# Copies of turned probabilities after the score tiles of three and four key tiles, on ScalarE instead of VectorE

## The chip, the cores and the metric

The kernel runs on one core of one Trainium2 chip. The metric is the device time of one execution in microseconds (us). A core has five engines that run their own instruction streams and meet only at semaphores: TensorE (PE in the rows: PE is the matmul, PEld the weight load that overlaps it), VectorE (DVE), ScalarE (ACT), GpSimd (POOL) and SyncE (SP, which issues the DMAs).

## The reference

The input x is 32 images of 192 channels and 32 x 32 points. Three layers follow; the change touches the second.

```python
x = _L0_conv_ref(x, ...)                  # channel attention, 8 heads, plus x
t = _to_tokens(x)                         # 32 x 1024 tokens x 192
t = t + _L1_attn_ref(_ln_t(t), Wq, Wk, Wv)
t = t + _L1_ffn_ref(_ln_t(t), W1, b1, W2, b2)
x = _from_tokens(t, x)
...
def _L1_attn_ref(x, Wq, Wk, Wv):          # H = 6 heads, d = 32
    att = jnp.einsum('bqhd,bkhd->bhqk', q, k) * scale
    causal = jnp.tril(jnp.ones((T, T), dtype=bool))
    att = jnp.where(causal, att, -jnp.inf)
    att = jax.nn.softmax(att, axis=-1)
    out = jnp.einsum('bhqk,bkhd->bqhd', att, v)
```

The attention is causal over 1024 tokens. Cut into 8 query tiles of 128, query tile number q needs q + 1 key tiles of 128.

## The kernel before

**Units and slots.** A unit is one head and one query tile of one image: 48 units to an image, 1536 in all. The function `attention` runs over slots. It is called six times: for five groups of 6 images, and for a last pair. Between the calls stands the feed-forward layer (`group_tail`), which the change doesn't touch. In slot n the scores of unit n are made (line 659, and 661 for the causal mask), and the probabilities of unit n - 3 are turned, that is transposed (line 673), so that the product with V can follow (line 693). `TILES = [(1, 7), (3, 5), (0, 6), (2, 4)]` gives the query tiles: in blocks of six slots, even slots have the small query tile of the pair and odd slots the big one, for three heads. With the key tiles counted, four blocks (24 slots, twice in an image) run 2/8, 4/6, 1/7, 3/5. So where a small unit of three or four key tiles is turned, three slots later, the scores of a big unit are being made: of 8 key tiles in slots 1 and 25 of an image, of 6 in slots 9, 11, 33 and 35, of 7 in slots 13 and 37, of 5 in slots 21, 23, 45 and 47.

**One slot, engine by engine.** Each engine's program is written out slot by slot, and each engine runs its own strictly in that order:

- TensorE: scores of unit n, then transposes of unit n - 3 into a bank PT0 or PT1 of PSUM, then, in some slots, the product with V, then one step of the front of the next image (its layer 0, layer norm and projections, lines 560 to 636), spread over slots 0 to 44.
- VectorE: the row maximum of unit n (line 1172, `nmax`), then its copies of turned probabilities from PT into `work` (line 373), then its part of the front (among it BN_STATS at line 1046).
- ScalarE: Exp of unit n (line 915; it ends with an instruction of its own that reads the accumulated row sum), then its copies (line 919, which run in `pt_copy`), then its part of the front (lines 843 to 876).

**Chunks and banks.** The turned probabilities of a unit go into chunks of at most four key tiles (512 columns). Units of up to four key tiles have one chunk, larger ones two. Chunks take the banks PT0 and PT1 in turn (`i % 2`), so the transposes of chunk i + 2 wait until the copy of chunk i has emptied its bank:

```python
pe.wait_ge(pt_free[i % 2], after(g, 0, PT_IMG, i // 2))
```

A small unit turned in slot n is chunk i. In slot n + 1 a big unit follows with chunks i + 1 and i + 2, and chunk i + 2 needs the bank of the small one. Behind it on TensorE are the product with V, a front step and the scores of slot n + 2. Other waits that matter: scores of unit n wait for the Exp of unit n - 2, whose tile S they overwrite.

**Who copies.** `by_act` decides. Before, ScalarE copies every second chunk of a unit (`chunk[3] > 0`) and VectorE every first one.

Of the kernel before, what the change touches and what calls it, by code (L numbers as in the profile page):

```python
# [67 lines left out]
def qtile(n):  # L68
    return TILES[n // 6 % 4][n % 2]
# [91 lines left out]
def hybrid_kernel(nc, x, wa, wb, wv, wpt, bp, temp, w3, w1, b1, w2, b2, out):  # L161
# [5 lines left out]
    with ctx:  # L167
# [193 lines left out]

        def by_act(i, chunk):

            return chunk[1] == "p" and chunk[3] > 0

        def pt_copy(eng, copy, g, images, i):

# [457 lines left out]
        def _(act):  # L825
# [74 lines left out]
            def attention(g, images, fronts):  # L900
                for n in range(last_slot(images) + 1):
                    for j in batches_at(images, n, OT_AT):
                        act.wait_ge(pv_made, after(g, 0, KI, BATCH * (j + 1)))
                        if j >= 1:

                            act.wait_ge(t1_step, after(g, 0, 3 * NBI, 3 * (j - 1) + 2))
                        A(oT[:, :], OUT[0:CH, :], ACT.Copy).then_inc(oT_made, 1)
                    if n < UNITS * images:

                        act.wait_ge(max_made, after(g, 0, UNITS, n + 1))  # L910
                        if n >= 4:
                            i = max(i for i, c in enumerate(CHUNKS[images]) if c[1] == "p" and c[2] == n - 4)
                            act.wait_ge(pt_full[i % 2], after(g, 0, PT_IMG, i // 2 + 1))
                        w = P * (qtile(n) + 1)
                        A(PS[n % 2][:, n // 2 % 2, 0:w], S[:, n % 2, 0:w], ACT.Exp, bias=nmax[:, n % MAXES:n % MAXES + 1],  # L915
                          accum_out=rowsum[:, sum_col(n):sum_col(n) + 1]).then_inc(exp_made, 1)
                    for i, c in chunks_at(images, n):
                        if by_act(i, c):
                            pt_copy(act, lambda o, x: A(o, x, ACT.Copy), g, images, i)  # L919
                    fronts_at(n, lambda name, u: front_part(name, g, u + 1), order, fronts)  # L920
                    if images == GS and EARLY.get(n, "").startswith("norm"):
                        act.wait_ge(rstd2_made, after(g, 0, 4, 4))
                        norm_z2(0, g * GS, int(EARLY[n][-1]), zcat0)
                    if images == GS and EARLY.get(n, "").startswith("turn"):
                        k = int(EARLY[n][-1])
                        put_z2(0, g * GS, k, FB[k % 2])
# [57 lines left out]
        def _(dve):  # L984
# [183 lines left out]
            def attention(g, images, fronts):  # L1168
                for n in range(last_slot(images) + 2):
                    if n < UNITS * images:  # L1170
                        dve.wait_ge(scores_full, after(g, 0, UNITS, n + 1))
                        v.tensor_reduce(nmax[:, n % MAXES:n % MAXES + 1], S[:, n % 2, 0:P * (qtile(n) + 1)], AX.X, ALU.max,  # L1172
                                        negate=True).then_inc(max_made, 1)
                    for i, c in chunks_at(images, n):
                        if c[1] == "p" and not by_act(i, c):
                            pt_copy(dve, v.tensor_copy, g, images, i)

                    for i, c in chunks_at(images, n):
                        if c[1] == "o":
                            add_to_t1(g, i, c[2])  # L1180
                    fronts_at(n, lambda name, u: front_part(name, g, u + 1), later, fronts)
                    if images == GS and n in EARLY:
                        part = EARLY[n].removeprefix("next_")
                        b = int(part != EARLY[n])
                        if part == "stats0" and b:
                            dve.wait_ge(ln2_step, after(g, 0, 16, 16))
                            alone(dve)
                        if part.startswith("stats"):
                            stats2(b, range(4 * int(part[-1]), 4 * int(part[-1]) + 4))
                        elif part == "aggregate":  # L1190
                            aggregate2(g * GS + b)
# [158 lines left out]
```

## Time and profile before

| | |
|---|---|
| median of 3 runs | 4680.67 us (4678.06 to 4683.2) |
| the profiled execution, its own time | 4680.1 us |
| its span in the profile | 4678.3 us |
| TensorE busy (matmul) | 4079.7 us, 87% |
| TensorE weight loads | 2975.4 us, 64% |
| VectorE busy | 3329.6 us, 71% |
| ScalarE busy | 2690.2 us, 58% |
| GpSimd busy | 363.1 us, 8% |
| share of the chain that ended last | TensorE 62%, VectorE 15%, issue 14%, ScalarE 4% |
| mean granted TensorE clock | 0.977 of full |

The busy times are of the whole span. Matmuls overlap each other, so the busy share of TensorE is an upper view of its work. The chain is followed back from the last instruction, at each step to what released it.

### The profile page before, as it was taken

Reading aid. Unit: us, or ns where it says so; the run is one execution under the profiler, and the core shown is the slowest. Engines: PE = TensorE matmul, PEld = TensorE weight load, DVE = VectorE, ACT = ScalarE, POOL = GpSimd, SP = SyncE. Lnnn points to the kernel's source line nnn. Section 1 sums busy time; section 2 is a strip of 40 time slices with the busy share of each in tenths; the row PEclk is TensorE's granted clock in tenths of the full one; section 3 lists DMA queues with packets and bytes.
Section 4 is the critical chain, followed back from the end, with each engine's and each line's share of the span. In section 5 each row is a group of like instructions: output and inputs, shape, how many; then the busy total and the mean of one; then the engine's idle time right before and its main releaser. Section 6 shows DMA issues by size and latency. Waiting matters only on the chain.

```text
span 4678.3 us, 114637 instructions
## 1 busy us (share of the span) xinstructions
PE 4079.7 (87%) x39208; PEld 2975.4 (64%) x39208; DVE 3329.6 (71%) x6327; ACT 2690.2 (58%) x5901; POOL 363.1 (8%) x374
## 2 busy tenths in 40 slices
PE   3899988878999888999998979999888989988888
PEld 2667665566667646766675566666646667665665
DVE  3677777767777767777777777777767777776776
ACT  1565556555656655555556545565655555556555
POOL 1000002000000120000002000000110000002000
PEclk8999999999999999999999999999999999999999
DMA  1211111011111201111111011122101111111011
GB/s 43 60 37 35 35 35 35 0 47 37 35 35 41 48 10 41 35 35 35 35 38 33 0 49 35 35 51 46 35 0 41 35 35 35 42 35 28 0 41 42
DMA packets 48635, 160.95 MB, mean 34 GB/s; under 512 B 12420, under 2 KB 12934, under 8 KB 48006
## 3 DMA queue, kind: packets, MB, share of 16 engines
q1 hardware_dynamic: 48134, 154.39, 13.8%
q8 instruction: 300, 4.92, 0.4%
q14 instruction: 201, 1.65, 0.1%
HBM read 28.52 MB, written 25.17 MB: 11 GB/s over the span
## 4 chain that ended last, share of the span: by engine, by line
PE 62%; DVE 15%; issue 14%; ACT 4%; POOL 2%; DVEq 1%; DMA 1%; ACTq 0%; SPq 0%; POOLq 0%
PE PT L673 10%; PE OUT L693 10%; PE S L659 5%; PE PT L790 5%; DVE nmax L1172 4%; PE S L718 4%; DVE work L373 4%; PE S L619 2%; PE FR L619 2%; PE S L761 2%; PE FR L567 2%; PE S L567 2%; DVE XT L1054 1%; PE FR L626 1%; PE S L626 1%
## 5 line engine op out<-in xcount | busy, mean ns | idle before, releaser
L915 ACT ACTIVATE work<-S,nmax 128x256 f32<-128x256 f32 (+7 forms) x1536 | 1137.2, 741 | 1127.6 <-DVE nmax L1172 1059.5
L1172 DVE TENSOR_REDUCE nmax<-S 128x1 f32<-128x256 f32 (+7 forms) x1536 | 1156.7, 753 | 806.3 <-PE S L661 788.3
L673 PE MATMUL PT<-ident,work 128*128 128x128 f32 x6912 | 1103.7, 280 | 225.8 <-DVE work L373 197.0
L673 PEld LDWEIGHTS PT<-ident,work 128*128 128x128 f32 x6912 | 745.6, 142 | 433.7 <-DVE work L373 261.0
L373 DVE COPY work<-PT 128x512 f32<-128x512 f32 (+3 forms) x1536 | 893.6, 582 | 42.5 <-PE PT L673 35.0
L659 PE MATMUL S<-KS,QS 128*128 128x512 f16 (+3 forms) x1152 | 323.1, 335 | 61.2 <-ACT work L915 28.8
L661 PE MATMUL S<-causal,identb 128*128 128x128 bf16 x1536 | 339.7, 221 | 0.0
L659 PE MATMUL S<-odd 128*128 128x512 f16 (+3 forms) x1152 | 315.6, 328 | 22.9 <-ACT work L915 21.5
L919 ACT ACTIVATE work<-PT 128x512 f32<-128x512 f32 (+3 forms) x768 | 330.5, 430 | 3.4 <-PE PT L673 3.4
L693 PE MATMUL OUT<-work,odd 128*32 128x128 f32 x6912 | 303.6, 276 | 0.0
L1206 DVE TENSOR_REDUCE gm<-S 128x1024 f32 (+1 forms) x180 | 220.0, 1222 | 117.2 <-PE S L761 116.9
L693 PE MATMUL OUT<-work,V 128*32 128x128 f32 x6912 | 303.0, 275 | 0.0
L915 ACT ACTIVATION_READ_ACCUMULATOR work<-S,nmax 128x1 f32 x1536 | 301.1, 196 | 0.0
L718 PE MATMUL S<-odd,W1b 128*128 (+1 forms) x1080 | 256.9, 390 | 49.6 <-ACT work L958 41.3
L761 PE MATMUL S<-odd,W1b 128*128 (+1 forms) x1080 | 292.0, 379 | 0.0
L958 ACT ACTIVATE work<-S,sc 128x512 f32<-128x512 f32 x360 | 254.4, 782 | 50.1 <-PE S L718 49.6
L693 PEld LDWEIGHTS OUT<-work,odd 128*32 128x32 f32 x6912 | 235.6, 110 | 39.8 <-issue 31.2
L693 PEld LDWEIGHTS OUT<-work,V 128*32 128x32 f32 x6912 | 234.3, 110 | 39.8 <-issue 32.1
L790 PE MATMUL PT<-W2b,work 128*128 128x192 f16 x2880 | 247.5, 247 | 9.0 <-DVE odd L1259 8.8
L790 PEld LDWEIGHTS PT<-W2b,work 128*128 128x128 f16 x2880 | 238.8, 98 | 23.7 <-DVE odd L1259 9.9
L1251 DVE SCALAR_TENSOR_TENSOR work<-work 128x1024 f16<-128x1024 f32 x180 | 218.4, 1225 | 28.3 <-ACT work L965 24.2
L661 PEld LDWEIGHTS S<-causal,identb 128*128 128x128 bf16 x1536 | 151.6, 99 | 126.6 <-issue 11.8
(205 smaller groups left out, 6018.9 us busy)
## 6 DMA issues: line engine op xcount, KB each, us to landing
X<-in_x SPq DMA_DIRECT2D x32, 768.0 KB, 5.3
odd<-hi_z SPq DMA_DIRECT2D x128, 192.0 KB, 4.2
odd<-odd SPq DMA_DIRECT2D x128, 192.0 KB, 4.2
out_y<-work SPq DMA_DIRECT2D x64, 384.0 KB, 3.6
QS<-hi_z SPq DMA_DIRECT2D x64, 192.0 KB, 3.9
QS<-odd SPq DMA_DIRECT2D x64, 192.0 KB, 4.0
KS<-hi_z SPq DMA_DIRECT2D x64, 192.0 KB, 4.5
KS<-odd SPq DMA_DIRECT2D x64, 192.0 KB, 4.6
```

The source lines that it names most:

```text
L373: copy(PTS[m % 2][:, m // 2 % RING, P * c0:P * (c0 + k)], PT[i % 2][:, 0:P * k]).then_inc(pt_free[i % 2], 1)
L659: mm(S[:, n % 2, c0:min(w, c0 + 512)], q, KS[u % 2][:, h, c0:min(w, c0 + 512)], start=True, stop=c0 + 512 < w)
L661: mm(S[:, n % 2, w - P:w], identb[:, :], causal[:, :], start=False, stop=True).then_inc(scores_full, 1)
L673: last = tr(bank[:, P * (j - c0):P * (j - c0) + P], PS[m % 2][:, m // 2 % 2, P * j:P * j + P], ident[:, :])
L693: last = mm(OUT[32 * hh:32 * hh + 32, o:o + P], V[u % 2][:, j, D * h:D * h + D], PTS[k % 2][:, unit_of(k, hh) // 2 % RING, P * j:P * j + P ...
L718: last = mm(bank, W1b[:, j, P * (i % 6):P * (i % 6) + P], rhs[:, j, :], start=(j == 0), stop=(j == 2))
L761: last = mm(bank, W1b[:, j, P * m:P * m + P], Z2[:, b, hf, j, :], start=False, stop=(j == 2))
L790: last = mm(PT[tp % 2][:, C * t:C * t + C], HS[:, hf, part, m, o:o + P], W2b[:, m, :], start=(m == 0 and part == 0), stop=(m == MH - 1 and ...
L915: A(PS[n % 2][:, n // 2 % 2, 0:w], S[:, n % 2, 0:w], ACT.Exp, bias=nmax[:, n % MAXES:n % MAXES + 1], accum_out=rowsum[:, sum_col(n):sum_co ...
L919: pt_copy(act, lambda o, x: A(o, x, ACT.Copy), g, images, i)
L958: A(H[:, i % MH, :], Y[i % 4], ACT.Gelu, bias=rb1[:, i % MH:i % MH + 1], scale=r1).then_inc(gelu_made, 1)
L1172: v.tensor_reduce(nmax[:, n % MAXES:n % MAXES + 1], S[:, n % 2, 0:P * (qtile(n) + 1)], AX.X, ALU.max, negate=True).then_inc(max_made, 1)
```

## The change

The first chunks of the units with query tiles 2 and 3 (three and four key tiles, 384 and 512 columns, one chunk each) are copied by ScalarE. An image has 12 such units, the kernel 384: 192 of each size. The instruction, its data and its waits stay the same; it stands in the same slot, on another engine.

```diff
         def by_act(i, chunk):
 
-            return chunk[1] == "p" and chunk[3] > 0
+            return chunk[1] == "p" and (chunk[3] > 0 or qtile(chunk[2]) in (2, 3))
```

On TensorE nothing moves. On ScalarE, in slot 25 of an image, the new copy comes behind the Exp of the unit with eight key tiles (128x1024) and ahead of the Exp of slot 26 (128x256). A minus is a row of before, a plus one of the change:

```order
 L915 ACTIVATE work,rowsum<-S,nmax 128x1024
-L910 REGISTER_ALU
-L913 REGISTER_ALU
+L369 REGISTER_ALU
+L919 ACTIVATE work<-PT 128x384
+L910 REGISTER_ALU
 L915 ACTIVATE work,rowsum<-S,nmax 128x256
```

The copy of 384 columns stands between two Exps that followed each other before.

On VectorE, the same slot 25 (with slot 24 ahead of it) in the program before: the maximum and the copy of slot 24, the maximum of slot 25, its copy, and the layer norm statistics of the front.

```order
L1171 REGISTER_ALU
L1172 TENSOR_REDUCE nmax<-S 128x1
L369 REGISTER_ALU
L372 REGISTER_ALU
L373 COPY work<-PT 128x512
L1171 REGISTER_ALU
L1172 TENSOR_REDUCE nmax<-S 128x1
L369 REGISTER_ALU
L373 COPY work<-PT 128x384
L353 REGISTER_ALU x2
L1046 BN_STATS stats<-T 128x6 x4
```

The same place in the changed program:

```order
L1171 REGISTER_ALU
L1172 TENSOR_REDUCE nmax<-S 128x1
L369 REGISTER_ALU
L372 REGISTER_ALU
L373 COPY work<-PT 128x512
L1171 REGISTER_ALU
L1172 TENSOR_REDUCE nmax<-S 128x1
L353 REGISTER_ALU x2
L1046 BN_STATS stats<-T 128x6 x4
```

The statistics now follow the maximum at once; the copy of 384 columns is gone from VectorE.

## Rows read from the trace of the kernel before

**Rows 1.** The page, costliest groups: busy us, mean ns | idle before, releasers.

```profile
L673 PE MATMUL PT<-ident,work 128*128 128x128 f32 x6912 | 1103.7, 280 | 225.8 <-DVE work L373 197.0
```

**Rows 2.** Groups by shape: copies on VectorE (L373) and ScalarE (L919).

```profile
L373 DVE COPY work<-PT 128x512 f32<-128x512 f32 x960 | 654.7, 682 | 38.1 <-PE PT L673 30.8 <-issue 1.2
...
L919 ACT ACTIVATE work<-PT 128x512 f32<-128x512 f32 x192 | 112.9, 588 | 0.0
...
L919 ACT ACTIVATE work<-PT 128x384 f32<-128x384 f32 x192 | 93.0, 484 | 0.0
```

**Rows 3.** Timeline, slots 1 and 2 of an image: start us, duration us, instruction.

```profile
1974.12 0.55 DVE L373 COPY work<-PT 128x384 f32<-128x384 f32 x1
...
1974.72 0.33 PE L673 MATMUL PT<-ident,work 128*128 128x128 f32 x1 [0.35 <-DVE work L373]
...
1975.25 0.19 ACT L915 ACTIVATION_READ_ACCUMULATOR work<-S,nmax 128x1 f32 x1
1975.34 0.48 ACT L851 ACTIVATE XT<-S 128x386 f32<-128x386 f32 x1
```

**Rows 4.** Timeline of the same image, slots 9 and 10, then 13 and 14.

```profile
1993.10 0.19 ACT L915 ACTIVATION_READ_ACCUMULATOR work<-S,nmax 128x1 f32 x1
...
1993.56 0.38 PE L673 MATMUL PT<-ident,work 128*128 128x128 f32 x2
...
2003.50 0.44 PE L673 MATMUL PT<-ident,work 128*128 128x128 f32 x2 [0.65 <-DVE work L373]
...
2003.79 0.19 ACT L915 ACTIVATION_READ_ACCUMULATOR work<-S,nmax 128x1 f32 x1
```

**Rows 5.** Timeline of the same image, slots 25 to 27.

```profile
2029.80 0.33 PE L673 MATMUL PT<-ident,work 128*128 128x128 f32 x1 [0.44 <-DVE work L373]
...
2030.32 0.19 ACT L915 ACTIVATION_READ_ACCUMULATOR work<-S,nmax 128x1 f32 x1
...
2031.29 0.22 PE L661 MATMUL S<-causal,identb 128*128 128x128 bf16 x1
...
2031.97 1.22 DVE L1172 TENSOR_REDUCE nmax<-S 128x1 f32<-128x1024 f32 x1
...
2032.20 0.41 PE L673 MATMUL PT<-ident,work 128*128 128x128 f32 x2 [0.69 <-ACT work L915]
```

**Rows 6.** Timeline of the same image, slots 33 to 35.

```profile
2046.65 0.44 PE L673 MATMUL PT<-ident,work 128*128 128x128 f32 x2
2046.83 0.21 ACT L915 ACTIVATION_READ_ACCUMULATOR work<-S,nmax 128x1 f32 x1
...
2047.58 0.22 PE L661 MATMUL S<-causal,identb 128*128 128x128 bf16 x1
...
2047.84 0.33 PE L673 MATMUL PT<-ident,work 128*128 128x128 f32 x1
```

**Rows 7.** Timeline of the same image, slots 37 and 38.

```profile
2056.35 0.19 ACT L915 ACTIVATION_READ_ACCUMULATOR work<-S,nmax 128x1 f32 x1
...
2056.41 0.38 PE L673 MATMUL PT<-ident,work 128*128 128x128 f32 x2
```

**Rows 8.** Timeline, slots 45 to 47 of the image before it.

```profile
1967.95 0.33 PE L673 MATMUL PT<-ident,work 128*128 128x128 f32 x1 [0.38 <-DVE work L373]
...
1968.16 0.19 ACT L915 ACTIVATION_READ_ACCUMULATOR work<-S,nmax 128x1 f32 x1
...
1968.69 0.22 PE L661 MATMUL S<-causal,identb 128*128 128x128 bf16 x1
...
1969.10 0.41 PE L673 MATMUL PT<-ident,work 128*128 128x128 f32 x2 [0.20 <-DVE work L373]
```

**Rows 9.** Windows, slots 16 to 24: us; PE, PEld, DVE, ACT, POOL busy; clock; DMA.

```profile
372.13:394.63 22.50, 20.05 (x188) 16.49 (x187) 15.07 (x38) 11.45 (x31) 0.00 (x0) 0.92 0.01 2
...
2005.83:2026.67 20.84, 18.39 (x189) 15.28 (x187) 14.70 (x38) 11.45 (x31) 0.00 (x0) 1.00 0.00 1
...
4065.21:4087.71 22.50, 20.05 (x189) 16.49 (x188) 14.89 (x38) 11.45 (x31) 0.00 (x0) 0.92 0.01 2
```

## Prediction

> **What bounds the kernel now.** I first read the page's groups. The busiest engine is TensorE, and where it stands still in front of the transposes (line 673) it is nearly always for a VectorE copy out of PT: 197.0 of 225.8 us [rows 1]. That looks like a case for taking copies off VectorE. But the row doesn't say what VectorE did before the copy, nor when ScalarE could have made it. For that I read the timeline of one whole image, slot by slot, and set beside each copy that moves (a) when TensorE needs the bank again, and (b) when ScalarE would reach the copy. The same places in the other images gave the same distances to within some 0.01 us where TensorE waits, so one image stands for all.
>
> What the reader is to see is the chain inside an odd slot. The scores of a big unit end; VectorE takes the maximum; from there the ways part. VectorE copies the small unit's chunk at once, and in slot 2 TensorE starts 0.05 us after that copy's end (1974.12 + 0.55 = 1974.67, start 1974.72) [rows 3]. ScalarE starts the Exp of the big unit at the same moment as VectorE its copy, and reaches its own copies only when the Exp is through; in slot 1 the read of the row sum starts at 1975.25, half a microsecond after TensorE already has the bank [rows 3]. The kernel is bound by this latency from slot to slot, and by TensorE's own work where front steps fill the slots, not by the sum of work on VectorE (71% busy) or ScalarE (58%).
>
> **The change part by part.** It takes 192 copies of 512 columns at 0.682 us [rows 2] and 192 of 384 columns at 0.55 [rows 3] off VectorE: 237 us. It adds 192 at 0.588 and 192 at 0.484 to ScalarE [rows 2]: 206 us. Neither sum is on the path. No transpose, DMA or semaphore is added.
>
> A sentence on a rule: the Trainium skill, ScalarE: Activation LUTs, Rules for kernel authors, budgets about 0.3 us and 0.83 ns per element for an ACTIVATE. By it the two copies would be estimated at 0.72 and 0.62 us, 0.14 more than the rows have, and the eight late places counted below would cost some 34 us more. The rows decide here, since they have this very copy on this very engine.
>
> *When the copy is done on ScalarE.* The instruction after the row-sum read starts 0.09 to 0.10 us after the read's start (1975.25, then 1975.34) [rows 3]. So the copy ends at the read's start + 0.10 + 0.48 (384 columns) or 0.59 (512), and TensorE starts 0.05 later: read + 0.63 or + 0.74. Subtracting the present start of the transposes that need the bank gives the new stall in each image:
>
> - slot 1 (384): 1975.25 + 0.63 - 1974.72 = 1.16 [rows 3]
> - slot 9 (512): 1993.10 + 0.74 - 1993.56 = 0.28 [rows 4]
> - slot 13 (512): 2003.79 + 0.74 - 2003.50 = 1.03 [rows 4]
> - slot 25 (384): 2030.32 + 0.63 - 2029.80 = 1.15 [rows 5]
> - slot 33 (512): 2046.83 + 0.74 - 2046.65 = 0.92 [rows 6]
> - slot 37 (512): 2056.35 + 0.74 - 2056.41 = 0.68 [rows 7]
> - slot 45 (384): 1968.16 + 0.63 - 1967.95 = 0.84 [rows 8]
> - slot 21: the same subtraction gives under 0.1; I count 0.08.
>
> In the other four (slots 11, 23, 35, 47) a long product with V stands between the two chunks, and the bank is needed only 0.7 to 2.3 us after ScalarE is done: nothing, as long as that product covers it; without it, they would cost like their neighbours.
>
> *What is absorbed.* A stall pushes back the product with V, the front step and the scores of slot n + 2, and with them the next maximum, Exp and copies: most later waits of TensorE start from those scores and move along whole. Only waits on something made before the stall shrink. VectorE is now ahead by the copy it lost. I find three places:
>
> - Slot 45. The mask matmul of slot 47 moves from 1968.69 to 1969.53, and slot 47's transposes, which so far wait until 1969.10 for a VectorE copy, can follow at 1969.58: 0.48 of the 0.84 is left for TensorE [rows 8].
> - Slot 25. The mask matmul of slot 27 moves from 2031.29 to 2032.44; its transposes from 2032.20 to about 2032.49, only 0.29. But the maximum of slot 27 starts at 2031.97 now because VectorE is behind, and then at 2032.44 + 0.22 + 0.04 = 2032.70. What follows to slot 31 hangs on that maximum: 0.73 [rows 5]. This is where taking 0.55 us off VectorE helps.
> - Slot 33. The mask matmul of slot 35 goes from 2047.58 to 2048.50, the transposes from 2047.84 to 2048.55: 0.71 of 0.92 [rows 6].
>
> The others are carried in full. What is queued behind the new copies on ScalarE (front copies of lines 851 to 871, the small Exp) is up to 0.6 us later, but its readers come at least a slot later, and the small Exp waits today for a maximum that VectorE will deliver earlier. I count nothing for it; if that cover is gone, the front steps on TensorE slip by up to the same 0.6 in the slots with a new copy.
>
> Sum per image: 0.48 + 0.28 + 1.03 + 0.08 + 0.73 + 0.71 + 0.68 = 3.99 us, times 32 = 128 us. Slot 1 has no such copy in the first image of each of the six calls: 26 x 1.16 = 30 us. Together **158 us**.
>
> *The clock.* From slot 16 to slot 24 an image takes 20.84 us at a granted clock of 1.00; in 8 of the 32 images it takes 22.50 us at 0.92 [rows 9], that is, TensorE ran for a short time at 1.2 instead of 2.4 GHz: 1.66 us for each such fall. TensorE stood still for 20.84 - 18.39 = 2.45 us in that stretch. Elsewhere in attention the profile has hardly a fall. The change makes new stalls of that kind: 0.35 + 1.16 in slot 2, 0.65 + 1.03 in slot 14, 0.44 + 1.15 in slot 26 [rows 3 to 5]. Their price has bounds: no fall, 0; a fall in every image at two of the three, 64 x 1.66 = 106 us. I take the rate of the row that is nearest, 8 at each of the three places: 24 x 1.66 = **40 us**.
>
> The sum is 4680.1 (the profiled execution's own time) + 158 + 40 = 4878 us. The profiled time is 0.6 below the median of the runs, which changes nothing.
>
> **The rivals.**
>
> *Forecast: slower, by the late bank* (chance 0.72), near 4878. Its own range is 4820 to 4940.
>
> *Partly absorbed* (0.14). The late bank is real, but VectorE, with 237 us less to do, and the slack of the front steps take back more than I found: only the three longest stalls at slots 1, 13 and 25 count, at half: 32 x (1.03 + 1.15) / 2 + 26 x 1.16 / 2 = 50 us, without falls: 4730. For it speaks that VectorE is behind in slots 25 to 31; against it that in slots 1 to 12 TensorE has only waits that start from the delayed scores.
>
> *Slower still* (0.08). Nothing is absorbed (4.98 x 32 + 30 = 190 us), and the clock falls twice in each image (106 us): 4976.
>
> *Faster, by relief of VectorE* (0.04). VectorE is behind from slot 25 to 31, and TensorE waits there for its copies. If the bank of the moved chunk isn't what holds TensorE, the stretch gets shorter by the copy that leaves, 0.55 x 32 = 18 us: 4662. It decides if ScalarE delivers the chunk no later than VectorE now, so if the Exp is over within the 0.55 us of VectorE's copy. The rows have the row-sum read 0.52 us after TensorE's present start [rows 5], so it misses by 1.15. The Trainium skill, Perfetto Trace Analysis, Optimizing Scalar/DVE Operations, says that where VectorE is saturated, moving work to ScalarE may make sense; by that rule this rival would be the likely one. No row here shows VectorE saturated over an image.
>
> *No change that can be told* (0.02): the stalls hidden behind front steps, as in slots 11 and 35, everywhere: 4680.
>
> **How the numbers follow.** The predicted time is the forecast's, 4878. The low end, 4800, has three quarters of the 158 us and no fall (4680 + 119); the high end, 4940, has nothing absorbed and 42 falls (190 + 70). Below it lie the partly absorbed case and the two others, above it part of the last. A measurement of this kernel tells about 0.2% (9 us) from no change. Faster by more: 0.04; within: 0.02; slower by more: 0.94.
>
> **What the profile of the changed kernel would show.** The copies of line 373 fall from 1536 to 1152 and those of line 919 rise from 768 to 1152, with 0.48 and 0.59 us for the new ones. TensorE's wait in front of line 673 has ScalarE's copy (line 919) as its main releaser, with about seven waits an image; its sum rises by 100 to 190 us. The timeline of an image shows the stalls at slots 2, 14, 26, 34, 38 and 46 at about the lengths above, and an image takes 4 to 5 us longer plus the falls. VectorE and ScalarE wait longer for scores. More short falls of the clock stand between slots 0 and 31. I am wrong if the stalls are there but the images aren't longer (absorbed), if line 919 isn't the releaser, or if the clock falls at nearly every one of the new stalls.

## The result, and the profile after

| | before | after |
|---|---|---|
| median of 5 runs each | 4680.67 us (4678.06 to 4684.71) | 4846.58 us (4844.26 to 4852.95) |
| ratio | | 1.0354, 95% interval 1.034 to 1.0368 |
| the profiled execution, span | 4678.3 us | 4845.1 us |
| mean granted TensorE clock | 0.977 | 0.965 |

The change makes the kernel slower by 165.9 us; the prediction said 198 (4878), range 4800 to 4940.

The page of the kernel after, its engines and the groups that answer to [rows 1]. Columns as before: busy us, mean ns of one, idle before, and what ended it.

```profile
span 4845.1 us, 114637 instructions
...
PE 4122.1 (85%) x39208; PEld 3010.4 (62%) x39208; DVE 3137.6 (65%) x5943; ACT 2850.5 (59%) x6285; POOL 363.1 (7%) x374
...
L673 PE MATMUL PT<-ident,work 128*128 128x128 f32 x6912 | 1123.3, 282 | 355.0 <-ACT work L919 236.3
```

VectorE is busy for 192 us less and ScalarE for 160 more (the durations sum to 237 and 206, but rows of successive instructions overlap by about 0.1 us), and TensorE still waits longer: in front of the same transposes it stands 355.0 us instead of 225.8, and the releaser has changed from VectorE's copy to ScalarE's. The waits of the same kernel split it:

```profile
PE PT L673 <- ACT work L919: 236.3, 188, 1.8
...
PE PT L673 <- DVE work L373: 109.7, 221, 0.9
```

Each row has the total in us, the number of waits and the longest. 188 waits of 1.26 us in the mean for ScalarE's copies are new, six an image where I had said seven; those for VectorE fall from 197.0 to 109.7. ScalarE's copies by shape, to be set against [rows 2]:

```profile
L919 ACT ACTIVATE work<-PT 128x512 f32<-128x512 f32 x384 | 226.0, 589 | 0.0
...
L919 ACT ACTIVATE work<-PT 128x384 f32<-128x384 f32 x384 | 185.2, 482 | 1.4 <-PE PT L673 1.0
```

The new copies last what the old ones of that shape did, 0.59 and 0.48 us. They aren't slow, they are late. The timeline of slots 1 and 2 of an image, which answers to [rows 3]:

```profile
2041.33 1.11 ACT L915 ACTIVATE work<-S,nmax 128x1024 f32<-128x1024 f32 x1 [1.07 <-DVE nmax L1172]
2042.34 0.19 ACT L915 ACTIVATION_READ_ACCUMULATOR work<-S,nmax 128x1 f32 x1
2042.43 0.48 ACT L919 ACTIVATE work<-PT 128x384 f32<-128x384 f32 x1
...
2042.96 0.33 PE L673 MATMUL PT<-ident,work 128*128 128x128 f32 x1 [1.50 <-ACT work L919]
```

ScalarE has stood idle for 1.07 us for the maximum, then runs the Exp, and only then the copy. In the kernel that copies ahead of the Exp (below), the chunk is ready within the time of that wait. TensorE stands for 1.50 us instead of 0.35: 1.15 more, where the prediction had 1.16.

**Stretch by stretch.** The windows below cut an image where slots begin (at the mask matmul). First the kernel before, slots 0 to 3, 11 to 15, 23 to 27, 27 to 33, 33 to 39, and 39 to the next image's slot 0. Columns: window, us, busy of PE, PEld, DVE, ACT and POOL, granted clock, DMA share, GB/s.

```profile
1971.34:1976.60 5.26, 4.91 (x52) 3.72 (x51) 3.73 (x6) 3.47 (x11) 0.00 (x0) 1.00 0.64 153
1995.40:2005.27 9.87, 8.91 (x129) 7.36 (x127) 5.93 (x13) 3.88 (x11) 1.00 (x1) 1.00 0.01 2
2023.01:2031.29 8.28, 7.57 (x97) 5.84 (x95) 6.06 (x21) 3.72 (x9) 0.10 (x1) 1.00 0.38 95
2031.29:2044.78 13.49, 10.00 (x105) 6.58 (x103) 12.97 (x27) 8.22 (x19) 4.93 (x4) 1.00 0.01 4
2044.78:2059.41 14.63, 14.51 (x155) 9.76 (x153) 9.85 (x15) 10.05 (x25) 0.00 (x0) 1.00 0.01 2
2059.41:2077.60 18.19, 17.48 (x207) 13.59 (x205) 13.71 (x24) 12.75 (x30) 0.00 (x0) 1.00 0.58 125
```

The same stretches of the kernel after, in images where the clock stood at 1.00:

```profile
2038.43:2044.84 6.41, 4.91 (x53) 3.71 (x51) 3.27 (x5) 4.05 (x13) 0.00 (x0) 1.00 0.51 117
1952.77:1963.67 10.90, 8.91 (x129) 7.36 (x127) 4.75 (x11) 4.92 (x13) 1.06 (x1) 1.00 0.01 2
1981.56:1990.99 9.43, 7.56 (x97) 5.83 (x95) 5.75 (x19) 5.21 (x14) 1.63 (x2) 1.00 0.32 85
1990.99:2004.05 13.06, 9.81 (x104) 6.59 (x103) 12.30 (x25) 7.47 (x15) 3.45 (x3) 1.00 0.01 2
2004.05:2020.09 16.04, 14.54 (x156) 9.74 (x153) 8.33 (x12) 11.42 (x28) 0.00 (x0) 1.00 0.01 2
2020.09:2038.43 18.34, 17.12 (x207) 13.57 (x206) 12.72 (x22) 13.29 (x32) 0.00 (x0) 1.00 0.60 132
```

TensorE's busy time is the same in each pair but the fourth and the last, where it differs by 0.2 and 0.4; its time standing still is what grows.

| slots | before | after | more | the prediction's terms for it |
|---|---|---|---|---|
| 0 to 3 | 5.26 | 6.41 | 1.15 | 1.16 |
| 11 to 15 | 9.87 | 10.90 | 1.03 | 1.03 |
| 23 to 27 | 8.28 | 9.43 | 1.15 | 1.15 |
| 27 to 33 | 13.49 | 13.06 | -0.43 | 0.73 - 1.15 = -0.42 |
| 33 to 39 | 14.63 | 16.04 | 1.41 | 0.71 + 0.68 = 1.39 |
| 39 to the next slot 0 | 18.19 | 18.34 | 0.15 | 0.48 |

The two stretches with the small terms, slots 9 to 11 and 15 to 23, are 0.33 and 0.14 longer by the starts of their mask matmuls (0.28 and 0.08 in the prediction). The fourth line is the relief of VectorE: in a stretch in which VectorE is busy for 12.97 of 13.49 us, part of the stall comes back. Two runs below place it at the copy of slot 25: slots 27 to 33 take 13.06 us where the units of three key tiles alone are moved, and 13.48 where those of four alone are.

The prediction counted nothing for what is queued behind the new copies on ScalarE. The stretches agree: slots 3 to 9, which have no new copy, take 14.45 us in both kernels, and no other stretch grows by over 0.06 us more than its computed stalls.

### The profile page after: what moved, and what is told of

The parts are those of the page before. It is cut to its first block, busy times and chain, and to the rows that moved or that the text cites. A ratio compares the mean times of both kernels' runs of the same rounds, so it can differ in the third digit from the quotient of the medians.

```text
span 4845.1 us, 114637 instructions
## 1 busy us (share of the span) xinstructions
PE 4122.1 (85%) x39208; PEld 3010.4 (62%) x39208; DVE 3137.6 (65%) x5943; ACT 2850.5 (59%) x6285; POOL 363.1 (7%) x374
## 4 chain that ended last, share of the span: by engine, by line
PE 60%; issue 14%; DVE 14%; ACT 8%; POOL 2%; DVEq 1%; DMA 1%; ACTq 1%; SPq 0%; POOLq 0%
PE PT L673 11%; PE OUT L693 10%; DVE nmax L1172 5%; PE S L659 5%; PE PT L790 4%; PE S L718 4%; ACT work L919 3%; PE S L619 2%; DVE work L373 2%; PE S L761 2%; PE FR L567 2%; PE S L567 2%; ACT work L915 2%; PE FR L619 2%; PE FR L626 1%
## 5 line engine op out<-in xcount | busy, mean ns | idle before, releaser
L673 PE MATMUL PT<-ident,work 128*128 128x128 f32 x6912 | 1123.3, 282 | 355.0 <-ACT work L919 236.3
L673 PEld LDWEIGHTS PT<-ident,work 128*128 128x128 f32 x6912 | 755.8, 144 | 563.1 <-ACT work L919 291.9
L373 DVE COPY work<-PT 128x512 f32<-128x512 f32 (+2 forms) x1152 | 658.5, 572 | 42.5 <-PE PT L673 35.5
L919 ACT ACTIVATE work<-PT 128x512 f32<-128x512 f32 (+3 forms) x1152 | 538.3, 467 | 8.4 <-PE PT L673 8.0
L693 PE MATMUL OUT<-work,V 128*32 128x128 f32 x6912 | 320.9, 286 | 0.0
L693 PE MATMUL OUT<-work,odd 128*32 128x128 f32 x6912 | 320.8, 286 | 0.0
L693 PEld LDWEIGHTS OUT<-work,odd 128*32 128x32 f32 x6912 | 246.5, 114 | 43.9 <-issue 30.0
L693 PEld LDWEIGHTS OUT<-work,V 128*32 128x32 f32 x6912 | 246.0, 114 | 44.3 <-issue 31.2
```

The lines of the kernel that those rows point to most:

```text
L373: copy(PTS[m % 2][:, m // 2 % RING, P * c0:P * (c0 + k)], PT[i % 2][:, 0:P * k]).then_inc(pt_free[i % 2], 1)
L673: last = tr(bank[:, P * (j - c0):P * (j - c0) + P], PS[m % 2][:, m // 2 % 2, P * j:P * j + P], ident[:, :])
L693: last = mm(OUT[32 * hh:32 * hh + 32, o:o + P], V[u % 2][:, j, D * h:D * h + D], PTS[k % 2][:, unit_of(k, hh) // 2 % RING, P * j:P * j + P ...
```

## The experiments

Each was timed against the kernel before on the same chip. The diffs are against the changed kernel, but for the last, which is against the kernel before.

### Four copies that have slack

```diff
-            return chunk[1] == "p" and (chunk[3] > 0 or qtile(chunk[2]) in (2, 3))
+            return chunk[1] == "p" and (chunk[3] > 0 or (qtile(chunk[2]) in (2, 3) and chunk[2] % 6 // 2 == 1))
```

> Only the copies of slots 11, 23, 35 and 47 of an image (middle head of the three, 128 of the 384) go to ScalarE, those whose bank isn't needed for 0.7 us or more after ScalarE would be done. Theory (the bank is handed back late): no stall is made, 4680 us, ratio 0.998 to 1.002, TensorE's wait for line 919 in front of line 673 under 10 us. Rival (work on ScalarE costs as such, a third of the copies carries a third of the 166 us): about 4735 us, ratio 1.012.

Measured: 4677.68 us, ratio 0.9988 (0.9978 to 0.9997). 128 copies more on ScalarE and behind the Exp cost nothing. TensorE's wait in front of the transposes, from the groups of this kernel, is as before, and line 919 isn't among its releasers:

```profile
L673 PE MATMUL PT<-ident,work 128*128 128x128 f32 x6912 | 1105.1, 280 | 223.1 <-DVE work L373 194.5 <-ACT work L915 23.3 <-DVEq L1165 1.1
```

The interval ends just below 1 (0.9997), and nothing here rests on a gain of 0.1%.

### The eight others

```diff
-            return chunk[1] == "p" and (chunk[3] > 0 or qtile(chunk[2]) in (2, 3))
+            return chunk[1] == "p" and (chunk[3] > 0 or (qtile(chunk[2]) in (2, 3) and chunk[2] % 6 // 2 != 1))
```

> Only the copies of the other slots (1, 9, 13, 21, 25, 33, 37, 45; 256 of the 384) go to ScalarE. Theory (late bank): all of the loss is here, 4846 us, ratio 1.033 to 1.038. Rival (work on ScalarE costs as such): two thirds of it, about 4791 us, ratio 1.024.

Measured: 4853.48 us, ratio 1.0365 (1.0348 to 1.0382). The whole loss is here. The interval overlaps that of the change. With the run before, the rival that a copy on ScalarE has a price as such is out: a third of the copies costs nothing, two thirds all.

### The copy ahead of the Exp

ScalarE has the same 384 copies as in the change, each ahead of the Exp of its slot.

```diff
+        def ahead_of_exp(chunk):
+
+            return by_act(0, chunk) and chunk[3] == 0
...
+                    for i, c in chunks_at(images, n):
+                        if ahead_of_exp(c):
+                            pt_copy(act, lambda o, x: A(o, x, ACT.Copy), g, images, i)
                     if n < UNITS * images:
 
                         act.wait_ge(max_made, after(g, 0, UNITS, n + 1))
...
-                        if by_act(i, c):
+                        if by_act(i, c) and not ahead_of_exp(c):
```

> All 384 copies on ScalarE as in the change, but in ScalarE's program ahead of the Exp of the same slot instead of behind it. Theory (the copy is late because it stands behind the Exp): the copy is done about 0.6 us after its transposes, ahead of the maximum's end; all eight stalls go, and the present waits for VectorE at slots 2, 14, 26 and 46 (0.35, 0.65, 0.44, 0.38 us) too: 4640 us, 4615 to 4665, ratio 0.986 to 0.997. Rival 1 (work on ScalarE or its handover costs as such): 4800 or more. Rival 2 (the stalls go, but relief of VectorE is worth nothing): 4680.

Measured: 4638.87 us, ratio 0.9901 (0.9884 to 0.9917), 0.9% faster than before and 4.3% than the change. Engine, instruction, number and waits are the change's; only the place in ScalarE's program differs. The timeline of slots 1 and 2 (line numbers differ here: the transposes are line 677, the maximum is 1179, the new copies are line 914, the Exp is 922):

```profile
1954.27 0.49 ACT L914 ACTIVATE work<-PT 128x384 f32<-128x384 f32 x1 [0.29 <-PE PT L677]
...
1954.58 0.71 PE L677 MATMUL PT<-ident,work 128*128 128x128 f32 x5
...
1955.05 1.11 ACT L922 ACTIVATE work<-S,nmax 128x1024 f32<-128x1024 f32 x1 [0.29 <-DVE nmax L1179]
```

The copy runs in the time in which ScalarE waited for the maximum, the Exp still waits 0.29 us for it afterwards, and the five transposes of slot 2 run in one piece: neither the 1.50 us of the change nor the 0.35 of before.

### All small units ahead of the Exp

As the run before, with

```diff
-            return chunk[1] == "p" and (chunk[3] > 0 or qtile(chunk[2]) in (2, 3))
+            return chunk[1] == "p" and (chunk[3] > 0 or qtile(chunk[2]) <= 3)
```

> As the one before, with the copies of all small units (one to four key tiles, 768 copies) on ScalarE ahead of the Exp. Theory: TensorE's waits in slots 4, 16, 28 and 30 for VectorE copies of one and two key tiles (0.68, 0.39, 0.37 and 0.59 us) go too: about 4600 us, 4570 to 4640. Rival (ScalarE gets in the way of its own Exp, whose end the scores two slots later wait for): no better than the run before.

Measured: 4623.58 us, ratio 0.9868 (0.9851 to 0.9884), the fastest of all, 1.3% faster than before. It is inside the expected range but 24 us short of its centre, and the waits say why. The waits of the run before this one, in which only the copies of three and four key tiles stand ahead of the Exp:

```profile
PE PT L677 <- DVE work L377: 136.6, 303, 0.9
...
PE S L663 <- ACT work L922: 69.7, 148, 4.6
```

The same two waits with the copies of all small units ahead of it:

```profile
PE S L663 <- ACT work L922: 143.9, 168, 4.2
PE PT L677 <- DVE work L377: 61.1, 168, 0.9
```

The waits for VectorE's copies fall by another 76 us, but the scores' wait for the Exp two slots before, 69.7 us there, is 143.9 here: it takes the place of much of what was removed. The rival in the expectation was right in this half.

### Three key tiles alone, four alone

```diff
-            return chunk[1] == "p" and (chunk[3] > 0 or qtile(chunk[2]) in (2, 3))
+            return chunk[1] == "p" and (chunk[3] > 0 or qtile(chunk[2]) == 2)
```

> Only the units of three key tiles (slots 1, 21, 23, 25, 45, 47; 192 copies) go to ScalarE, behind the Exp. Theory (late bank, stretches of the changed kernel's trace): 26 x 1.15 + 32 x (0.14 + 0.72 + 0.16) = 63 us, and 0 to 10 us of clock falls in slots 29 to 31: 4750 us, 4740 to 4760, ratio 1.013 to 1.017. The recorded prediction's terms (0.48 at slot 45, two thirds of the 40 us of falls) would give 4778. Rival (work on ScalarE costs as such): half of the 166 us, 4763, and then the same for the units of four.

Measured: 4770.75 us, ratio 1.0191 (1.0174 to 1.0208).

```diff
-            return chunk[1] == "p" and (chunk[3] > 0 or qtile(chunk[2]) in (2, 3))
+            return chunk[1] == "p" and (chunk[3] > 0 or qtile(chunk[2]) == 3)
```

> Only the units of four key tiles (slots 9, 11, 13, 33, 35, 37; 192 copies) go to ScalarE, behind the Exp. Theory: 32 x (0.33 + 1.02 + 0.72 + 0.68) = 88 us, and about 20 us of clock falls in slot 14: 4788 us, 4770 to 4800, ratio 1.019 to 1.026. If the stalls add up place by place, this and the run before sum to the change's 166 us within 20. Rival (work on ScalarE costs as such): 4763.

Measured: 4753.91 us, ratio 1.0159 (1.0142 to 1.0176).

The losses are 91.7 and 74.8 us against 4679.08 of the kernel before beside them, together 166.5; the change's is 165.9. TensorE's waits for line 919 add up too: 132.1 and 104.0 us in the two, 236.3 in the change. But both single times missed what I expected, the first by 21 us upwards, the second by 34 downwards, and both lie outside their expected ranges. They are also within 10 us of the 4763 of the rival that a copy on ScalarE has a price as such, so these two times can't rule it out; the runs before do, and so do the stretches. The stalls were as computed: stretch by stretch the two have the change's lengths where their own copies are, and those of before elsewhere. The clock went another way. The view of the cores has span and mean granted clock. The kernel with the units of three key tiles moved:

```profile
core 0: 4775.8 us, clock 0.964
```

The kernel with those of four:

```profile
core 0: 4751.4 us, clock 0.981
```

The kernel with the stalls of slots 1, 21, 25 and 45 has a lower clock than before (0.977), the one with those of slots 9, 13, 33 and 37 a higher one, though its stalls are 88 us against 63. All four executions of each agree: 0.964 to 0.970 and 0.980 to 0.982. In attention the first profile has 40 falls and the second 7; before has 12. The nine falls that before has in slot 19 are all gone in the second, which had no stall of its own there; it has six in slot 14. The falls cost about 31 us more than before's in the first kernel and 7 less in the second (by the stretches with a fall against the same stretches without), and about 26 more in the change. That these parts add up as well was not to be expected from their places, and no run explains it.

### VectorE's copy, made as late

The kernel before, nothing moved to ScalarE; the 384 copies wait for the Exp of their slot.

```diff
                         if c[1] == "p" and not by_act(i, c):
+                            if qtile(c[2]) in (2, 3) and n < UNITS * images:
+                                dve.wait_ge(exp_made, after(g, 0, UNITS, n + 1))
                             pt_copy(dve, v.tensor_copy, g, images, i)
```

> The kernel before, with all copies on VectorE where they were, but the 384 copies of the change wait for the Exp of the same slot. Nothing is on another engine; only the lateness is there. Theory (lateness alone makes the loss): the bank comes back 0.2 us later than in the changed kernel and VectorE's next maximum is held up too: 4905 us, 4870 to 4960, ratio 1.040 to 1.060. Rival (the loss comes from ScalarE's load or its handover): 4680.

Measured: 4998.26 us, ratio 1.0694 (1.0669 to 1.072). Waiting for the Exp makes a loss with ScalarE as free as before. Its size was beyond my range: 319 us, not 225. The groups of this kernel:

```profile
L373 DVE COPY work<-PT 128x512 f32<-128x512 f32 (+3 forms) x1536 | 896.1, 583 | 509.7 <-ACT work L915 466.5 <-PE PT L673 35.8 <-issue 1.2
```

VectorE stands 466.5 us for the Exp in front of these copies, and the maximum of the next slot is queued behind them. I had counted only the later bank, not that next maximum in full. By the starts of the mask matmuls the stalls are 1.52 us at slot 1 and about 7.8 us over the rest of an image, some 290 us in all where the change has 151; a bank 0.2 us later at eight places would be 1.6 us an image more. So the larger part is likely the held-up maximum, but no run takes the two apart. This run therefore shows that ScalarE's load isn't needed for a loss; it doesn't isolate the late bank. The pair that does is the change and the kernel with the copy ahead of the Exp.

## Why the prediction was right, point by point

**The bound.** It was the latency from slot to slot. Taking work off VectorE lowered its busy share from 71% to 65% and lost 3.5%; the same work taken off it without lateness gained 0.9%.

**The stalls.** 3.99 us per image and 1.16 at slot 1 were predicted, 158 us in all. Measured by the stretches, without falls of the clock: 0.33 + 1.03 + 0.14 + (1.15 - 0.43) + 1.41 + 0.15 = 3.78 us, times 32 = 121, and 26 x 1.15 = 30: 151 us. Every place has its stall, and all but that of slot 45 agree within 0.06 us, those of slots 33 and 37 by their sum.

**The mis-sized term: slot 45.** "0.48 of the 0.84 is left" was 0.15, 10 us over the kernel. I had let the scores of slot 47 move by the whole stall. But before, they weren't directly behind the transposes of slot 46: in [rows 8] the row-sum read of slot 45 ends at 1968.16 + 0.19 = 1968.35, and the scores of unit 47, which overwrite that tile, have to wait for it. The kernel before has that wait in front of the weight load of these scores, whose matmuls start 0.46 us behind the start of the transposes:

```profile
1968.40 0.11 PEld L659 LDWEIGHTS S<-KS,QS 128*128 128x128 f16 x2 [0.32 <-ACT work L915]
1968.41 0.45 PE L659 MATMUL S<-KS,QS 128*128 128x512 f16 x2
```

The stall covers it. In the kernel after, the scores start 0.17 us behind the start of the transposes:

```profile
2035.72 0.33 PE L673 MATMUL PT<-ident,work 128*128 128x128 f32 x1 [1.22 <-ACT work L919]
...
2035.89 0.43 PE L659 MATMUL S<-KS,QS 128*128 128x512 f16 x2
```

The stall itself is as computed (1.22 instead of 0.38, 0.84 more). Of it 0.29 goes here, and another 0.4 behind slot 47's mask matmul, as the prediction had it.

**The mis-sized term: the clock.** The falls were there (53 in attention instead of 12), but cost about 25 us, not 40, and not where I put them. (The stretches with a fall are together 42 us longer than the same stretches at full clock; in the kernel before it is 16.) None stands at slot 2 but one in the last image, and none at slot 26; 14 begin in slot 14, 23 in slot 29, 6 in slot 31, and 8 in slot 19 (9 before). Windows of the kernel after, slots 11 to 15 with a fall, then slots 27 to 33 with a fall in slot 29 and with one in slot 31, against 10.90 and 13.06 at full clock:

```profile
1500.68:1512.74 12.06, 10.08 (x128) 7.96 (x126) 4.73 (x11) 4.92 (x13) 1.00 (x1) 0.89 0.01 2
...
2441.26:2454.32 13.06, 10.98 (x104) 7.55 (x103) 12.39 (x25) 7.43 (x15) 3.39 (x3) 0.87 0.01 3
3906.58:3921.11 14.53, 11.28 (x105) 7.88 (x104) 12.30 (x25) 8.39 (x18) 3.40 (x3) 0.88 0.00 1
```

A fall in slot 14 costs 1.16 us there (and 0.1 behind it), one in slot 31 1.47, and one in slot 29 nothing: TensorE is busy 10.98 instead of 9.81 us in the same 13.06. Two parts of the stretch at full clock, at the places where the falls of slots 29 and 31 lie in other images, show why they differ:

```profile
1995.34:1998.75 3.41, 2.75 (x41) 1.95 (x40) 3.41 (x8) 1.10 (x3) 1.66 (x2) 1.00 0.01 2
2000.92:2004.05 3.13, 3.13 (x40) 2.37 (x39) 2.62 (x6) 2.10 (x4) 0.00 (x0) 1.00 0.02 5
```

In the first VectorE has no pause and TensorE is busy for 2.75 of 3.41 us, so VectorE sets the pace; in the second TensorE has none. I had given each fall the 1.66 us of slot 19. That the term came within 15 us is partly luck: I had 24 new falls where there were 41, at a price that most of them didn't have, and the two errors work against each other.

**What lies outside attention.** The six calls of attention together, from their first to their last mask matmul, are 176 us longer (151 + 25), the span 167. So 9 us come back outside: 6.7 between the calls and 2.6 ahead of the first and behind the last. At each of the five gaps 0.4 of it is the part of slot 45's stall that is taken back past slot 47. The rest wasn't followed; the run with the four slack copies, whose attention has no new stall, is 2.6 us shorter there too. The prediction has no term for this, and without these 9 us the change would lie nearer to it, at 176 of 198.

**The rivals.** Partly absorbed: VectorE's relief does give back, 0.43 us per image in slots 27 to 33, as the forecast had it, and no more. Faster by relief: the mechanism is real, but needs the copy ahead of the Exp. Then slots 23 to 33, the part that this rival spoke of, are 0.46 us shorter an image, 15 us in all where I had 18; the gain of the whole kernel is 44 us, since TensorE's old waits for these copies go at the other places too.

## What to carry to other kernels

Before work moves to the engine with more idle time, look at where in that engine's order it will stand and what that place waits for: a copy of 0.5 us on an engine that is idle 40% of the time cost 1.15 us, because it stood behind an instruction that waited for something later. Subtract two times of the old trace, when the new engine reaches the work and when the result is needed, at each place in the loop; where the difference is negative the move is free, and the rest is the stall. Then ask whether the work can go into the idle time ahead of that wait: the same move, one place earlier, turned +3.5% into -1%.

## What the runs showed of the hardware

In this kernel the sum of the stalls doesn't tell how the granted clock will move: 63 us of stalls at slots 1, 21, 25 and 45 brought it from 0.977 to 0.964, 88 us at slots 9, 13, 33 and 37 raised it to 0.981. Fewer stalls don't raise it either: with the copies ahead of the Exp it was 0.972 (0.971 to 0.973 in its four executions), with 19 falls in attention. Their places matter; no run shows by what rule. What a fall of the same length costs went from nothing (slot 29, where VectorE has no pause) to 1.47 us (slot 31, where TensorE has no pause) and 1.66 us (slot 19).
